# The recurrent mixer's weights loaded and scaled in the stage before it, and the first scaling of that stage put ahead of the second group's statistics

## What is computed

```
h = h + _L0_attn_ref(_layernorm(h), W_qkv, conv_w, W_z, W_b, W_a, dt_bias, A_log, norm_weight, W_out)
# inside:
mixed = silu(causal_conv(hidden @ W_qkv.T, conv_w))      # 2048 channels, 4 taps
z     = hidden @ W_z.T                                     # 1024 channels
beta  = sigmoid(hidden @ W_b.T)
g     = -exp(A_log) * softplus(hidden @ W_a.T + dt_bias)
... recurrence over the rows, 16 heads of 64 ...
h_ = o * silu(z);  h_ = h_ * rsqrt(mean(h_ * h_) + EPS) * norm_weight
return h_ @ W_out.T
```

## Time and profile before

| what | value |
|---|---|
| median of 3 executions | 3087.56 us (3084.33 to 3089.98) |
| the profiled execution, its own time | 3085.63 us |
| its span in the profile | 3083.9 us |
| prepare, from SP's first load to DVE's last gate operation | 739.4 to 800.4 us |
| from there to the mixer's first DMA issue | 800.4 to 802.6 us |
| from that issue to the mixer's first matmul | 802.6 to 821.2 us |
| PE busy in the span | 2436.0 us (79%) |
| DVE busy in the span | 2084.8 us (68%) |

### The profile page before, as it was taken

How to read it: one execution, slowest core, us unless ns; L and a number is a source line. 1 busy time by engine, 2 the same in 40 slices (tenths; PEclk the granted TensorE clock), 3 DMA queues, 4 the chain that set the end, 5 groups by cost and what they waited for, 6 DMA issues and landing times. The chain is left out here.

```text
span 3083.9 us, 53608 instructions
## 1 busy us (share of the span) xinstructions
PE 2436.0 (79%) x19286; PEld 1864.6 (60%) x19286; DVE 2084.8 (68%) x5004; ACT 1244.2 (40%) x2990; POOL 815.8 (26%) x644
## 2 busy tenths in 40 slices
PE   7888887997458888888888888876452847889698
PEld 5666665886446666666666666655341735566454
DVE  4777774333368888888888888855563336876663
ACT  1334342221256566666666666642000213344132
POOL 2111100001033232232222333221377036450110
PEclk9999998997579999999999999988665877899799
DMA  4210001002201111211122211111211852110000
GB/s 141 72 62 27 12 9 45 21 27 75 100 19 46 49 49 49 50 49 50 49 50 49 50 49 49 46 46 30 88 45 21 263 176 63 45 51 4 18 25 25
DMA packets 274346, 169.01 MB, mean 55 GB/s; under 512 B 182847, under 2 KB 250318, under 8 KB 273728
## 3 DMA queue, kind: packets, MB, share of 16 engines
q1 hardware_dynamic: 247949, 140.28, 15.9%
q0 software_dynamic: 26112, 25.03, 3.1%
HBM read 99.23 MB, written 73.45 MB: 56 GB/s over the span
## 5 line engine op out<-in xcount | busy, mean ns | idle before, releaser
L1187 POOL TENSOR_TENSOR qd<-decay,qm 114x456 f32<-114x456 f32 x128 | 143.4, 1141 | 638.3 <-DVE qm L1280 492.5
L1601 PE MATMUL d_ps<-d_xT,w_qkv 128*128 128x228 f32 x1024 | 236.8, 391 | 44.7 <-DVE qmask L1395 29.2
L1601 PEld LDWEIGHTS d_ps<-d_xT,w_qkv 128*128 128x128 f32 x1024 | 217.2, 213 | 77.1 <-issue 43.2
L2256 POOL DMA_INDIRECT s_eo<-rows_y,slots_all x128 | 152.4, 1191 | 148.3 <-POOLq L87 110.3
L1248 DVE TENSOR_TENSOR elim_tmp<-ue 128x30 f32<-128x30 f32 (+14 forms) x480 | 178.8, 372 | 13.8
L1250 DVE TENSOR_TENSOR ue<-ue,elim_tmp 128x30 f32<-128x30 f32 (+14 forms) x480 | 171.9, 358 | 16.5
L475 PE MATMUL t_ps<-xT,w_qk 128*128 128x154 f32 x1024 | 151.1, 300 | 40.3 <-DVE qk L308 30.9
L1589 PE MATMUL d_ps<-gl,after 114*114 114x456 f32 x256 | 137.2, 654 | 47.2 <-DVE sz L1335 47.2
L1322 DVE SCALAR_TENSOR_TENSOR y_v<-raw,taps,y_v 128x228 f32<-128x228 f32 x384 | 167.1, 508 | 10.6 <-ACT y_v L1452 10.5
L475 PEld LDWEIGHTS t_ps<-xT,w_qk 128*128 128x128 f32 x1024 | 136.7, 189 | 51.8 <-DVE qk L308 38.1
L1206 POOL TENSOR_SCALAR_AFFINE_SELECT ue<-ue 128x1024 f32<-128x1024 f32 x16 | 98.6, 6162 | 238.1 <-DMA ue<-blocks_n 238.1
(11 more groups left out here) (343 smaller groups left out, 5625.0 us busy)
## 6 DMA issues: line engine op xcount, KB each, us to landing
rows_x<-zero_row SPq DMA_DIRECT2D x4, 2048.0 KB, 7.7
ue<-blocks_n SPq DMA_DIRECT2D x16, 512.0 KB, 4.9
blocks_u<-ue SPq DMA_DIRECT2D x16, 512.0 KB, 2.6
blocks_v<-on SPq DMA_DIRECT2D x16, 512.0 KB, 2.7
e_x<-rows_x SPq DMA_DIRECT2D x32, 256.0 KB, 4.3
e_gu<-L_ffn_w_gate_up SPq DMA_DIRECT2D x32, 256.0 KB, 4.3
rows_y<-e_y SPq DMA_DIRECT2D x32, 256.0 KB, 3.4
blocks_n<-nt SPq DMA_DIRECT2D x96, 64.0 KB
```

Of the source, the lines that this page charges most:

```text
L1187: pool.tensor_tensor(qd[p.par][s][:, hs(u), :].rearrange("p (a o b) t -> p a o b t", o=2, b=2)[:, :, o], e[o][:, :, :].rearrange("p (a b) ...
L1601: last = pe.matmul(ps[:, f % 2, (t % 2) * W:(t % 2 + 1) * W], w_qkv[:, k, t * 128:(t + 1) * 128], xT[:, k, :], start=(k == 0), stop=(k == ...
L2256: pool.indirect_dma_start(out=eo[n % EO][:, s * TOPK + k, :], out_offset=None, in_=rows_y, in_offset=bass.IndirectOffsetOnAxis(ap=slots_al ...
```

## The change

1. The mixer's tiles `w_qkv`, `w_z`, `w_out`, `taps`, `gain` and `qmask` are allocated before prepare, and handed to it. prepare's SP issues the seven transfers (now on a semaphore `mix_in`) in group 3, right behind load 7 and ahead of store 3. prepare's DVE makes `qmask` behind the last `gate_read`, waits for the seven, and halves `taps` and `w_z`. SP waits for them at the end of the stage.
2. In the mixer the seven transfers, the waits for them and the three DVE operations are gone. DVE and ACT wait for the first memset alone, PE for neither. SP loads the first pair's `d_xT` first and zeroes `blocks_n` second.
3. In prepare scale(0) stands ahead of stat(1). The wait of DVE and of PE for the gate weights moves from their start to the first use (gate_read(0) and gate(0)).

```diff
@@ prepare, SP @@
+                def load_mixer():
+                    for dst, src in (
+                        (w_qkv[:, :, :], dr["L0_attn_W_qkv_t"].rearrange("(k p) n -> p k n", p=128)),
+                        (taps[:, :, :], dr["L0_attn_conv_w_c"]),
+                        (w_z[:, :, :], dr["L0_attn_W_z_t"].rearrange("(k p) n -> p k n", p=128)),
+                        (gain[0:DH, :], dr["L0_attn_norm_weight"].unsqueeze(1)),
+                        (gain[DH:128, :], dr["L0_attn_norm_weight"].unsqueeze(1)),
+                        (w_out[:, 0:4, :], dr["L0_attn_W_out_t"].rearrange("(k p) n -> p k n", p=128)[:, 0:4, :]),
+                        (w_out[:, 4:8, :], dr["L0_attn_W_out_t"].rearrange("(k p) n -> p k n", p=128)[:, 4:8, :]),
+                    ):
+                        sp.dma_start(dst, src).then_inc(mix_in, 16)
...
                     if g + HB < GROUPS:
                         sp.wait_ge(gxn_ready, g + 1)
                         load(g + HB)
+                    if g + HB == GROUPS - 1:
+                        load_mixer()
                     sp.wait_ge(gxT_ready, g + 1)
                     sp.dma_start(xts[:, :, g * L:(g + 1) * L], xT[g % 2][:, :, :]).then_inc(xT_out[g % 2], 16)
                 for n in range(2):
                     sp.wait_ge(xT_out[n], 16 * (GROUPS // 2))
+                sp.wait_ge(mix_in, 112)
@@ prepare, DVE @@
                 def gate_read(g):
+                    if g == 0:
+                        dve.wait_ge(gw_in, 64)
...
                 stat(0)
-                dve.wait_ge(gw_in, 64)
                 for g in range(GROUPS):
-                    if g + 1 < GROUPS:
+                    if g and g + 1 < GROUPS:
                         stat(g + 1)
                     scale(g)
+                    if g == 0:
+                        stat(1)
                     if g >= 2:
                         gate_read(g - 2)
                 gate_read(GROUPS - 2)
                 gate_read(GROUPS - 1)
 
+                ch.note(dve.tensor_scalar(qmask[:, :], c.upto[:, :], -DH ** -0.5, None, ALU.mult))
+                dve.wait_ge(mix_in, 112)
+                ch.note(dve.tensor_scalar(taps[:, :, :], taps[:, :, :], 0.5, None, ALU.mult))
+                ch(dve.tensor_scalar(w_z[:, :, :], w_z[:, :, :], 0.5, None, ALU.mult))
                 dve.wait_ge(ab_read, 2 * GROUPS)
@@ prepare, PE @@
-                pe.wait_ge(gw_in, 64)
...
                 def gate(g):
+                    if g == 0:
+                        pe.wait_ge(gw_in, 64)
@@ delta_net, SP @@
+                load_x(Pair(0, 0))
                 sp.dma_start(nd.rearrange("s h q j i -> (s h q) (j i)").rearrange("p (a d) -> p a d", d=D),
                              c.zero_row[:, :].unsqueeze(1).to_broadcast([128, 4, D])).then_inc(nd_zero, 16)
-                load_x(Pair(0, 0))
-                for dst, src in (
...
-                    sp.dma_start(dst, src).then_inc(dw_in, 16)
@@ delta_net, DVE @@
-                dve.wait_ge(dw_in, 16 * DW)
-                dve.wait_ge(d_init, INIT)
-                ch(dve.tensor_scalar(taps[:, :, :], taps[:, :, :], 0.5, None, ALU.mult))
-                ch(dve.tensor_scalar(w_z[:, :, :], w_z[:, :, :], 0.5, None, ALU.mult))
-                dve.tensor_scalar(qmask[:, :], c.upto[:, :], -DH ** -0.5, None, ALU.mult).then_inc(d_init, 1)
-                dve.wait_ge(d_init, INIT + 1)
+                dve.wait_ge(d_init, 1)
@@ delta_net, ACT @@
-                act.wait_ge(dw_in, 16 * DW)
-                act.wait_ge(d_init, INIT + 1)
+                act.wait_ge(d_init, 1)
@@ delta_net, PE @@
-                pe.wait_ge(dw_in, 16 * DW)
-                pe.wait_ge(d_init, INIT + 1)
```

More of the change, by code:

```diff
@@ L834, in _, with prepare @@
                     last.then_inc(o_mm, 1)
-def prepare(c, hid, xts, gates):
+def prepare(c, hid, xts, gates, w_qkv, w_z, w_out, taps, gain, qmask):
     nc, dr = c.nc, c.dram
@@ L853, in prepare @@
         ps = ctx.enter_context(nc.psum_tensor("g_ps", [128, 6, 512], F32))
-        (gw_in, gvar_ready, grstd_ready, gxn_ready, g_t, gxT_ready, ab_mm, ab_read, abs_done, log1p_done, g_dve, g_act) = (
+        (gw_in, gvar_ready, grstd_ready, gxn_ready, g_t, gxT_ready, ab_mm, ab_read, abs_done, log1p_done, g_dve, g_act, mix_in) = (
             c.sem(n) for n in ("gw_in", "gvar_ready", "grstd_ready", "gxn_ready", "g_t", "gxT_ready", "ab_mm",
-                               "ab_read", "abs_done", "log1p_done", "g_dve", "g_act"))
+                               "ab_read", "abs_done", "log1p_done", "g_dve", "g_act", "mix_in"))
         h_in = [c.sem(f"g_h_in{n}") for n in range(HB)]
@@ L1034, in delta_net @@
         gates = sb("gates", [S, B, 2 * H])
-        c.stage(prepare, hid, xts, gates)
         w_qkv, w_z, w_out = sb("w_qkv", [128, KD, 2048]), sb("w_z", [128, KD, 1024]), sb("w_out", [128, 8, D])
         taps, gain, qmask = sb("taps", [128, CT, TAPS]), sb("gain", [128, 1]), sb("qmask", [S, S])
+        c.stage(prepare, hid, xts, gates, w_qkv, w_z, w_out, taps, gain, qmask)
         xT, xz = sb("d_xT", [128, KD, W]), sb("d_xz", [128, KD, W])
@@ L1052, in delta_net @@
         ps = ctx.enter_context(nc.psum_tensor("d_ps", [128, 8, 512], F32))
-        (dw_in, d_init, xT_in, xz_in, nd_zero, nd_out, ue_in, ud_out, ut_in, qkv_mm, raw_r, tap_r, conv_r, th_r, yy_r,
+        (d_init, xT_in, xz_in, nd_zero, nd_out, ue_in, ud_out, ut_in, qkv_mm, raw_r, tap_r, conv_r, th_r, yy_r,
          kq_mm, qm_r, gl_r, dec_mm, e_r, nt_r, qd_r, sel_r, elim_r, z_mm, thz_r, sz_r, vt_mm, p_mm, rc_r, t_mm, xc_r,
@@ L1057, in delta_net @@
             c.sem("d_" + s) for s in (
-                "w_in", "init", "xT_in", "xz_in", "blocks_zeroed", "blocks_out", "blocks_in", "inverse_out", "inverse_in",
+                "init", "xT_in", "xz_in", "blocks_zeroed", "blocks_out", "blocks_in", "inverse_out", "inverse_in",
                 "qkv_mm", "raw_ready", "tap_ready", "conv_steps", "th_ready", "silu_ready", "kq_mm", "qmasked_ready",
@@ L1065, in delta_net @@
         h_out = [c.sem(f"d_h_out{s}") for s in range(2)]
-        DW = 7
         INIT = 5
```

## The result

Six executions of each kernel on one chip gave a median of 3071.6 us (3066.0 to 3078.65) against 3087.89 us before (3084.33 to 3089.98). The ratio on record is 0.9961 (95% interval 0.9943 to 0.9978), that is -12 us, with -7 to -18 us in the interval. It is not the quotient of the two medians, which is 0.9947 (-16.3 us) and also lies in that interval; what follows goes by the ratio. The forecast was -6.5 us (3081.1 us, ratio 0.9979). So the sign was right, but the gain measured in this comparison is nearly twice the forecast, which lies just outside the interval. The median of 3071.6 us is inside the range given (3071.0 to 3086.0) by 0.6 us, and outside the forecast's own part of it (3078 to 3085).

The account below looks back on a forecast made before the run. Bound by the mixer's initial DMA wait for weights and prepare's queue on six or seven DMA engines. -15.3 + 8.8 + 0 = -6.5 us, giving 3081.1 us; range 3071.0 to 3086.0, the forecast's own 3078 to 3085.

Parts of the forecast that it names:

- What bounds the stretch: Mixer's start: PE idle 29.2 us in a DMA wait; prepare: loads on six or seven DMA engines form a queue.
- Part 1: Mixer's start: without the weight transfers PE starts 3.3 us after SP's first issue instead of 18.59, a gain of 15.3 us.
- the clock costs as before: Mixer's first projections: PE's half-speed start stays as it was; the possible further gain of some 1.6 us is not counted.
- Part 2: Prepare: weights queued ahead of store 3 delay it and copy 5, so prepare ends 8.8 us late.
- Copy 5: Prepare, group 5's copy: waits for store 3 and starts at about 788.9 instead of 776.90, 12.0 us late.
- DVE's three operations: End of prepare: taps, w_z and qmask, together 1.8 us, fit where DVE is idle for ACT, so cost nothing.
- Part 3: Prepare's front: scale(0) first turns group 0 3.9 us earlier, but turn(1) still waits on loads; gain 0 us.
- 435 GB/s: Weights in prepare at the ceiling rate: 9.7 us, a loss of 6.1 and a sum of -9.2 us.
- the row that the prediction went by: Weights' earlier landings at the mixer's start: 12.4 us for 4128 KB, or 341 GB/s, giving the sum of -6.5 us.
- Rival A: Prepare: the stores are not held up by the weights, so the whole 15.3 us stay: 3072.3 us; chance 0.15.
- Rival B: Prepare: weights move at 138 GB/s, taking 30.6 us; prepare ends 27.0 us late, net +11.7, 3099.3 us; chance 0.06.
- Rival C: Mixer's start: d_xT or another engine comes 3 to 6 us later; net -3 to 0, about 3086 us; chance 0.04.

Follow-up runs that it names:

- Experiment 1: Changed kernel with the seven weight transfers issued behind store 5 instead of ahead of store 3: 66.0 us from load 0 to the mixer's first matmul, ratio 0.9962.
- experiment 2: Changed kernel with w_qkv loaded a second time ahead of store 3: 81.3 us from load 0 to the mixer's first matmul, ratio 1.0003.
- experiment 3: Kernel before with only scale(0) ahead of stat(1) and the gate-weight waits moved: 82.1 us from load 0 to the mixer's first matmul, ratio 0.9998.
- experiments 3 and 4: Experiment 3, and the changed kernel with stat(1) ahead of scale(0) again: 75.4 us from load 0 to the mixer's first matmul, ratio 0.9987.
- experiment 6: Experiment 1 with each load of hid cut into 112 partitions and 2: 62.6 us from load 0 to the mixer's first matmul, ratio 0.9925.
- experiments 6 and 7: Experiment 6, and the same with stat(1) ahead of scale(0) again: 63.4 us from load 0 to the mixer's first matmul, ratio 0.9921.
- second comparison: Changed kernel timed once more, unaltered, against the kernel before: 75.6 us from load 0 to the mixer's first matmul, ratio 0.9976 (0.9960 to 0.9991).

## Why the prediction was right, and where not

**What bounds the stretch.** Right. PE's wait for the weights at the mixer's start, and a queue of six engines or so under prepare. Experiment 1 moved only the place in the queue, and got back 9.6 us; experiment 2 lengthened what is in front of the store, and lost 5.7.

**Part 1, -15.3 us.** Right: first matmul 3.2 us after SP's first issue, forecast 3.3. Experiment 1 has nothing lost in prepare and so measures this term nearly by itself: 81.8 - 66.0 = 15.7 us, of which 15.4 lie between SP's first issue and the first matmul and 0.3 in prepare. The sentence "the clock costs as before" was wrong: not only did none of the possible 1.6 us come, the first 64 matmuls took 1.0 us longer (14.95 us against 13.97; 15.1 in experiment 1, 14.1 in experiment 3 with the old start). This is outside the local time, and was made up for by the mixer's first store of `nt` (-6.5 us there).

**Part 2, +8.8 us.** Right in its place and nearly in size: 75.6 - 66.0 = 9.6 us. Copy 5 was forecast 49.5 us from load 0 and came at 50.2. How it came about was forecast in part only. Store 3 was to take about 17 us to land, and took 11.7: SP, held up by the issues of the weights, issued it 9.1 us later than before, and only the rest of the delay stands in its landing (7.6 us before). PE's gap ahead of gate(5) was 7.3 us and not 9, for turn(6) was late as well. Also left out was that the weights slow down the transfer ahead of them. Load 7, issued 25.8 us after load 0 (26.0 before), let its statistics start at 38.7 us instead of 36.3, with DVE idle 2.52 us for it. That delayed turn(6), but not the end: PE still had to wait for copy 5 behind it. Where the 0.7 us between 49.5 and 50.2 come from is open. DVE's three operations were covered, and stores 4 and 5 came in time, as forecast.

**Part 3, 0 us.** Right, in experiments 3 and 4, and for the reason given, in experiment 6. In a kernel with quicker loads it is worth 0.8 us (experiments 6 and 7).

**Row and rule.** The Trainium skill's rule that each engine takes the descriptors of a ring in order ("DMA: Bandwidth & Descriptors", "Queues, rings and completion order") gave the sign of part 2, and experiments 1 and 2 agree, as does the order of the landings (`w_out` 786.4, store 3 787.7). The 435 GB/s that the prediction took from "Where 436 GB/s comes from" on the same page of the skill would have made it -9.2 us. But that section of the Trainium skill also says that between HBM and SBUF a lower figure binds, about 358 GB/s; by it, an estimate, the 4128 KB take 11.8 us and the sum is -7.1. The local time, -6.2, is on the side of the row that the prediction went by; for single stretches the rows show more than 358 GB/s as well (375 in the earlier trace rows), and there the measurement decides.

**Rival A**, no stall, falls: copy 5 starts at 50.2 us and not at 37.5. Experiment 1 makes it true, by another place for the weights. **Rival B** falls: store 3, with all 4128 KB ahead of it, landed 11.5 us after the statistics that waited for load 7 (776.18 to 787.7), not 30 us. **Rival C** falls: the wait at the mixer's start is 3.2 us.

**The size of the whole.** Local -6.2 against a forecast of -6.5. The first comparison's -12 us holds more than the change, as far as the runs show. That its median fell into the stated range is luck: the range reaches down to 3071.0 us for the sake of rival A, which did not come true. The second comparison gave -7.4 with an interval that the forecast lies well inside, and one visible part of the excess, the clock dip in the last stage, came and went in the same kernel. The mixer's time from its first to its last projection was 1135.8 us before, 1132.7 in the first profile after and 1131.8 in the second. These 3 to 4 us need not be the change's: in experiment 3, where the mixer starts as before, it was 1133.1, and in the other kernels it ran from 1128.7 to 1137.6. How the rest of the first -12 us comes about is open. What the prediction had too small was its allowance for scatter: 2 to 3 us for a median. On the second chip single executions of the kernel before ran from 3069.7 to 3103.9.

## What to carry to other kernels

A transfer moved into a busy stage doesn't take free bandwidth, it takes a place in a queue: look at who is behind it and what waits for that, and at what the issuing engine gets to too late, and issue it behind the last transfer on which the stage still depends. Here that was two groups later, and made 6.2 us into 15.7. Look also at how many DMA engines a tile's partition count allows, and judge an edit of a few us by the time between two fixed events around it, not by the whole. Put the second event far enough behind: here the first matmuls after the shorter wait ran 1.0 us longer.

## What was not expected of the hardware

- SP's issue of a DMA can take far longer than usual: `w_qkv` took 3.65 us to issue and the two halves of `w_out` 5.75 us in the changed kernel, against 0.62 us for `w_qkv` behind store 5. In the changed kernel it followed load 7 within 0.3 us. That a full queue is the reason was not tried.
- In the changed kernel, where PE is idle for 13.53 us and not 29.21 ahead of the mixer's first matmul, its granted clock stayed at 0.50 for the first 4 us (0.62 in the mean before), and the first 64 matmuls took 14.95 us instead of 13.97.
- Transfers behind a load delayed it by at least 2.4 us (load 7 above; before, DVE did not wait for it), though they stand behind it in the queue.
- The same stretch of the factorised MLP was granted 0.96 and 0.83 of PE's full clock in two executions of one kernel.
- One masking operation of POOL on 128x1024 elements (L1206) varies tenfold within one execution, as far as the profile's rough spans on POOL can say; row of the kernel before, shortest, median and longest in ns:

```profile
L1206 POOL TENSOR_SCALAR_AFFINE_SELECT ue<-ue x16: 1271/3482/13424, 896.8 to 2061.9; 128x1024 f32<-128x1024 f32 x16
```

Whether the mixer's scatter comes from it was not tried.
